# Softmax attention on one core: the products with v in runs of two or three groups, with 18 slots for the exponentials

## What is computed

```python
qkv = x @ w_qkv                       # x (4, 1024, 128)
q, k, v = split into 16 heads of D = 8
scores = einsum('bhqd,bhkd->bhqk', q, k) / sqrt(D)
scores = where(causal, scores, -inf)
out = einsum('bhqk,bhkd->bhqd', softmax(scores), v)
return out @ w_out
```

## Time and profile before

| | us |
|---|---|
| median of 3 runs | 1469.22 (1468.04 to 1473.21) |
| the profiled execution | 1472.18 |
| its span | 1470.5 |
| softmax attention's units on PE in it | about 76 to 580 |
| one unit, from one turning of the maxima to the next | 31.78 |
| granted TensorE clock in the middle units | 1.00 of full speed |

### The profile page before, as it was taken

How to read it: one execution, slowest core, us unless ns; L and a number is a source line. 1 busy time by engine, 2 the same in 40 slices (tenths; PEclk the granted TensorE clock), 3 DMA queues, 4 the chain that set the end, 5 groups by cost and what they waited for, 6 DMA issues and landing times. The chain is left out here.

```text
span 1470.5 us, 33772 instructions
## 1 busy us (share of the span) xinstructions
PE 1281.0 (87%) x10608; PEld 738.8 (50%) x10609; DVE 979.5 (67%) x2119; ACT 642.1 (44%) x1280; POOL 536.1 (36%) x615
## 2 busy tenths in 40 slices
PE   6699999999999996799999999999999977299990
PEld 4233333334333332356556565746565645299980
DVE  6868888877888881247584848485857556366656
ACT  4155556565556655242433334242524231155553
POOL 7112232323232322005261616253444434244456
PEclk9589999999999999799999999999999988599995
DMA  6452111111111110321121303030303050232215
GB/s 190 114 179 54 38 39 36 45 46 48 41 38 36 37 39 21 100 54 40 46 67 30 82 27 86 14 98 14 98 12 87 2 156 2 73 96 65 65 55 173
DMA packets 91756, 93.59 MB, mean 64 GB/s; under 512 B 16816, under 2 KB 77104, under 8 KB 91568
## 3 DMA queue, kind: packets, MB, share of 16 engines
q1 hardware_dynamic: 73872, 74.91, 18.7%
q0 software_dynamic: 9184, 13.39, 3.1%
q10 hardware_dynamic: 8640, 4.53, 1.1%
HBM read 49.84 MB, written 22.63 MB: 49 GB/s over the span
## 5 line engine op out<-in xcount | busy, mean ns | idle before, releaser
L1320 ACT ACTIVATE arena<-banks 128x512 f32<-128x512 f32 x576 | 302.4, 600 | 231.9 <-PE banks L1231 231.3
L1367 DVE TENSOR_REDUCE arena<-banks 128x4 f32<-128x512 f32 (+3 forms) x336 | 347.7, 1057 | 77.3 <-PE banks L1209 71.9
L1206 PE MATMUL banks<-arena 96*128 96x512 bf16 (+3 forms) x768 | 207.8, 344 | 25.7 <-DVE arena L1367 19.0
L424 PE MATMUL banks<-arena,h 128*128 128x512 f32 x512 | 226.7, 593 | 2.4 <-DVEq L369 1.0
L1231 PE MATMUL banks<-arena 99*128 99x512 bf16 (+3 forms) x768 | 176.7, 330 | 16.3 <-ACT arena L1320 11.3
L1488 POOL TENSOR_SCALAR_AFFINE_SELECT arena<-arena 128x512 f32<-128x512 f32 x128 | 79.9, 636 | 241.5 <-ACT arena L1320 241.4
L1256 PE MATMUL banks<-arena 128*32 128x512 f32 (+3 forms) x1536 | 156.8, 496 | 4.4 <-POOL arena L1488 2.7
L424 PEld LDWEIGHTS banks<-arena,h 128*128 128x128 f32 x512 | 94.7, 190 | 110.0 <-issue 105.0
L570 ACT ACTIVATE arena<-banks,sh 128x512 f32<-128x512 f32 x64 | 44.0, 687 | 214.4 <-PE banks L424 214.4
L1206 PEld LDWEIGHTS banks<-arena 96*128 96x128 bf16 x768 | 71.6, 101 | 125.8 <-DVE arena L1367 82.9
L440 POOL TENSOR_TENSOR arena<-arena 128x4 f32<-128x4 f32 x24 | 24.4, 1019 | 278.1 <-DVE arena L438 278.1
(11 more groups left out here) (162 smaller groups left out, 1947.9 us busy)
## 6 DMA issues: line engine op xcount, KB each, us to landing
arena<-arena SPq DMA_DIRECT2D x160, 128.0 KB, 2.3
arena<-k_parts SPq DMA_DIRECT2D x96, 96.0 KB
arena<-rows SPq DMA_DIRECT2D x72, 65.0 KB
arena<-q_parts SPq DMA_DIRECT2D x64, 64.0 KB
arena<-best SPq DMA_DIRECT2D x16, 256.0 KB, 4.6
k_parts<-arena SPq DMA_DIRECT2D x24, 128.0 KB, 3.0
arena<-q_parts SPq DMA_DIRECT2D x32, 96.0 KB
q_parts<-arena POOLq DMA_DIRECT2D x18, 128.0 KB, 3.0
```

Source lines behind the costliest of these rows:

```text
L424: ins = nc.tensor.matmul(dst, l, r, start=(n == 0), stop=(n == len(pairs) - 1), skip_group_check=True)
L1206: ins = nc.tensor.matmul(dst, sq[p][0:MROW, h, qt * P:(qt + 1) * P], sk[p][0:MROW, h, k0:k0 + n], start=True, stop=not diag, skip_group_ch ...
L1320: nc.scalar.activation(pe_[:, s % NSLOT, :], score[s % NBANK], ACT.Exp, scale=SCALE0)\
L1367: nc.vector.tensor_reduce(mx[:, 1 if k0 else 0, qt, hs[0]:hs[-1] + 1], src, AX.X, ALU.max)\
```

## The change

The products with v are no longer done one group at a time. `VALUES` says where and which: in group 0 those of groups 7, 8 and 9 of the unit before, in group 3 those of 0, 1 and 2, in group 5 those of 3 and 4, in group 7 those of 5 and 6. They stand at the same place within the group, after the two halves of the scores and the items between. After the last unit the products of its groups 7, 8 and 9 follow. The exponentials have 18 slots instead of 12. `norm` starts one `top` later in group 0, and in group 4 (after its first `top`) instead of in group 3 (after its second).

```diff
-NSLOT = 12
+NSLOT = 18
+VALUES = {0: [7, 8, 9], 3: [0, 1, 2], 5: [3, 4], 7: [5, 6]}
...
-            def times_v(u, p, g):
+            def times_v(u, p, groups):
+
+                for g in groups:
+                    group_v(u, p, g)
+
+            def group_v(u, p, g):
...
-                    if g or not first:
-                        times_v(*((u, p, g - 1) if g else (u - 1, 1 - p, NG - 1)))
+                    if g in VALUES and (g or not first):
+                        times_v(*((u, p) if g else (u - 1, 1 - p)), VALUES[g])
...
-            times_v(NU - 1, 1, NG - 1)
+            times_v(NU - 1, 1, VALUES[0])
...
-                    if g == 3:
+                    if g == 4:
                         pending = norm(u, 0)
...
-                        if (g, n) not in ((0, 0), (3, 0)):
+                        if (g, n) not in ((0, 0), (0, 1)):
                             next(pending, None)
```

## The result

The changed kernel takes 1556.28 us (median of 4 runs, 1553.83 to 1557.76), the kernel before 1468.84 (4 runs). The ratio is 1.0587, with a 95% interval of 1.0562 to 1.0612: slower by 87 us. The forecast was 1509, 40 us over, and its range ended at 1522. The direction was right, the size less than half of what was measured.

The account below looks back on a forecast made before the run. PE sets the pace, with DVE close to full. 2.66 us more in each of 14 units (37.2), 0.7 before and 2.2 in unit 15 make 40.1, so 1469.22 + 40 = 1509 us, range 1488 to 1522.

Parts of the forecast that it names:

- no change of mode is paid within a run: PE, products of neighbouring groups in a row: 10 pairs of changes become 4, 1.42 us less a unit.
- slots that cost nothing: Exponentials: the 6 more slots cost nothing, as each slot is freed a whole group or more before.
- the new waits for ACT: Groups 8 and 9: without products behind score 33, score 34 waits for ACT until 1.65 and score 35 until 2.14.
- for DVE at items 2 and 7 to 11: Groups 9 and 1 to 3: item 2 waits for item 0's reduction until 3.76; item 7 comes at 11.25, before 10.15.
- for the maxima: Before score 0: PE waits for the maxima's DMAs until 5.04, standing 0.94 us.
- The walk: One unit stepped through by prices from the earlier timeline, from score 30 at 0 to the next at 34.4, before 31.78.
- item 20: Groups 6 and 7: item 20 ends at 30.49, with score 26 there.
- new waits less changes of mode: Per unit: about 4.1 us lost in new waits, 1.42 won by changes, so 2.66 more.
- Its bounds: Range: the maxima's 4.16 (-13), handing over between engines (7 either way), and 5 more upwards where DMAs meet.
- only the changes of mode: Rival 1, whole kernel: waits don't grow, only changes of mode count, 1446.4 us; chance 0.07.
- a balance: Rival 2, whole kernel: new waits eat just the gain of 1.42 a unit, 1469 us; chance 0.06.
- 3: Rival 3, before score 0: the maxima's DMAs aren't late, a unit is 0.94 shorter, 1496 us; chance 0.2.

Follow-up runs that it names:

- the split: Changed kernel with two of the four small DMAs of the maxima issued by GpSimd, beside SP's two: 1535.38 us.
- the doubled scores: Score matmuls issued twice into the same bank: changed kernel, scores 4 to 9, 1515.42 us; scores 22 to 27, 1551.66; kernel before, scores 4 to 9, 1468.20.
- the partial kernels: Kernel before with 18 slots and only some products in a row: 7, 8, 9, 1498.03 us; 0, 1, 2, 1490.81; 3, 4 and 5, 6, 1469.09.
- the run with the transposes in the gaps: Changed kernel with norm's first transpose moved into DVE's idle gaps in groups 0 and 4: 1511.51 us.

## Why the prediction was wrong

**What held.** The direction; that no change of mode is paid within a run (1280 columns at full clock take 341.40 - 339.10 = 2.30 us, forecast 2.28); slots that cost nothing; the new waits for ACT, for DVE at items 2 and 7 to 11, and for the maxima, each at its place and up to item 9 within 0.1 us. Items 12 and 13, which I had behind DVE too, don't wait for it, since PE is at half clock there.

**What failed.** The sum used prices "all at a granted clock of 1.00", taken from the kernel before, for a kernel in which PE has longer and more waits. Nothing in the prediction asked what that does to the clock, and no rival stood for it. So the term of the lower clock stood at nothing without a reason; measured, it is 2.49 us a unit, in 14 units 35 us. Two smaller terms were off as well. The walk gave the product of `norm` 0.19 us of DVE's time, and it took 0.57 (346.27 to 346.84), which item 10 shows as 0.35. And item 20 waits 0.26 for DVE (the row at 365.45), where the walk had no wait and its end 0.45 too early; at full clock 0.30 of that reaches the turning.

| one unit against the kernel before | us |
|---|---|
| forecast: new waits less changes of mode | 2.66 |
| item 20 | 0.30 |
| product of `norm` | 0.35 |
| lower clock | 2.49 |
| the unit before is 31.70 in the mean, not 31.74 | 0.04 |
| sum, as measured: 37.54 - 31.70 | 5.84 |

Times 14 that is 81.8 us between the second and the last turning. With 0.2 up to the second (forecast 0.7) and 3.6 behind the last one (forecast 2.2) it is 85.6, which is the difference of the spans (1556.1 - 1470.5). At full clock the change costs 3.35 us a unit, where I had 2.66.

The range failed with the missing term. Its bounds held only what I could misread in the handing over, and were 12 us wide upwards. Of the rivals, 1 and 2 (only the changes of mode, or a balance) are excluded by the result, and 3 by the wait of 0.74 in the timeline and by the split. The savings on changes of mode alone would have given 1446; they are there, and the new waits are larger.

Shown by runs: that the lower clock costs 2.5 us a unit (intervals with and without it in one trace, and the doubled scores); that the doubled scores help only where the clock falls (not in groups 6 and 7, not in the kernel before); that DVE's chain and the maxima's DMAs are two separate costs. Open: what exactly decides whether the clock falls. The low stretches don't come in all units of the partial kernels, nor in two units whose PE work ahead of the place was the same, and I can't say from the rows in which they will.

## What to carry to other kernels

Work that looks like an interruption may be the filler that lets other engines catch up. Before putting it in a row, walk one period with the starts of the timeline and ask at each place who fills the bank or frees it; and put what the other engine can do (here the transposes) into the gaps that the run makes. When a change thins out PE's work anywhere in a loop, give the lower clock a rival of its own. As an estimate, its price is at most half of the stretch, what PE would have saved at full clock: 3.4 us for the 6.83 here, of which 2.5 showed. And look in the trace for units that escaped the lower clock: they give its price without another run.

## What was unexpected of the hardware

- The clock fell in 14 of 15 units, in group 2, for 6.83 us, though no single wait of PE was longer than 0.8 us; 1.3 us of useless matmuls a unit took all of these stretches out of group 2 and 36 us off the kernel.
- The same float32 product of DVE (L1414, SBUF to SBUF) took 0.28 us in some places and 0.65 in others. In the changed kernel it started at 346.27, and POOL was masking:

```profile
345.55 1.22 POOL L1494 TENSOR_SCALAR_AFFINE_SELECT arena<-arena 128x512 f32<-128x512 f32 x2 [5.00 <-ACT arena L1326]
```

Masking beside it isn't enough to make it slow. With scores 4 to 9 doubled it took 0.27 in the midst of two masks:

```profile
332.60 1.27 POOL L1494 TENSOR_SCALAR_AFFINE_SELECT arena<-arena 128x512 f32<-128x512 f32 x2 [5.22 <-ACT arena L1326]
333.11 0.27 DVE L1414 TENSOR_TENSOR arena<-arena 128x128 f32<-128x128 f32 x1
```

The traces differ in how long the mask that was under way still ran when the product started: 0.51 us in the changed kernel (that mask had begun 0.13 before) and 0.13 with the doubled scores. In both the product ended 0.14 us after the end of that mask. Two units with other distances agree: at 120.8 in the changed kernel the mask ran for 0.59 more and the product took 0.73, at 121.9 with the doubled scores 0.21 and 0.36. So the product seems to be held until the mask under way is done; no run tried this by itself. In the run with the transposes in the gaps and in the steady units of the kernel before, no mask runs beside it, and it takes 0.28.
